# Masked attention over gathered tokens: each batch's token order made three batches ahead, beside the batch's mean, in place of all orders in the first batch

## The reference

```python
xt = jnp.transpose(x, (0, 2, 1))
qh = (xt @ Wq.T).reshape(B, T, 8, 64).transpose(0, 2, 1, 3)
scores = scale * jnp.einsum('bhqd,bhkd->bhqk', qh, qh)
logits = (scores * cmask + (1.0 - cmask) * NEG) * rmask
ctx = jnp.einsum('bhqk,bhkd->bhqd', jax.nn.softmax(logits, axis=-1), qh)
out = x + jnp.transpose(ctx.transpose(0, 2, 1, 3).reshape(B, T, D) @ Wo.T, (0, 2, 1))
```

## Time and profile before

| | before |
|---|---|
| median of 3 runs | 1604.44 us (1604.06 to 1607.05) |
| the profiled execution | 1601.72 us |
| its span, first to last instruction | 1599.9 us |
| instructions | 33099 |
| PE / DVE / ACT / POOL busy | 1526.0 / 1189.8 / 852.9 / 1340.2 us |
| share of the span | 95% / 74% / 53% / 84% |
| mean granted TensorE clock | 0.984 of 2.4 GHz |

### The profile page before, as it was taken

How to read it: one execution, slowest core, us unless ns; L and a number is a source line. 1 busy time by engine, 2 the same in 40 slices (tenths; PEclk the granted TensorE clock), 3 DMA queues, 4 the chain that set the end, 5 groups by cost and what they waited for, 6 DMA issues and landing times. The chain is left out here.

```text
span 1599.9 us, 33099 instructions
## 1 busy us (share of the span) xinstructions
PE 1526.0 (95%) x10956; PEld 1215.0 (76%) x10956; DVE 1189.8 (74%) x2676; ACT 852.9 (53%) x2061; POOL 1340.2 (84%) x1078
## 2 busy tenths in 40 slices
PE   5889999999999999999999999999999999999985
PEld 4668787777878777787777878778787877877763
DVE  4586787878778787877878787787877778787763
ACT  4335555565555556555555556556555555645451
POOL 3466889898998989889898988989898898988885
PEclk9879999999999999999999999999999999999998
DMA  4433454454544445444445544444544444443411
GB/s 137 104 78 90 101 126 103 129 124 110 127 105 122 107 130 123 111 120 112 116 112 130 124 106 119 114 119 113 129 121 108 116 118 119 112 125 93 113 58 55
DMA packets 93810, 179.09 MB, mean 112 GB/s; under 512 B 24704, under 2 KB 24832, under 8 KB 93632
## 3 DMA queue, kind: packets, MB, share of 16 engines
q1 hardware_dynamic: 64448, 109.71, 29.7%
q0 software_dynamic: 29184, 67.17, 14.8%
HBM read 36.77 MB, written 33.55 MB: 44 GB/s over the span
## 5 line engine op out<-in xcount | busy, mean ns | idle before, releaser
L977 DVE TENSOR_REDUCE small_mxp<-max_scores 108x1 f32<-108x270 f32 x1280 | 547.0, 435 | 267.2 <-PE max_scores L1218 244.5
L827 ACT ACTIVATE small_Pt<-scores,small_kbias 108x270 f32<-108x270 f32 x1280 | 550.5, 482 | 362.2 <-PE scores L1237 356.8
L640 POOL TENSOR_TENSOR small_Pacc<-small_Pacc,small_Pt 108x540 f32<-108x540 f32 x384 | 518.8, 1351 | 119.7 <-ACT small_Pt L827 113.2
L1218 PE MATMUL max_scores<-small_ops 128*108 128x270 f32 x1280 | 417.0, 332 | 17.1 <-DVE small_mxp L977 15.4
L1249 PE MATMUL ctx_psum<-small_Pt,small_V 108*64 108x270 f32 x2560 | 314.0, 392 | 0.0
L1009 DVE RECIPROCAL small_rsum<-small_rsum 128x67 f32<-128x67 f32 (+1 forms) x512 | 240.7, 532 | 70.3 <-ACT small_rsum L763 67.1
L1218 PEld LDWEIGHTS max_scores<-small_ops 128*108 128x108 f32 x1280 | 220.1, 174 | 86.6 <-issue 42.1
L1234 PE MATMUL scores<-small_ops 128*108 128x270 f32 x1280 | 271.0, 292 | 2.7 <-ACT small_Pt L827 2.7
L1249 PEld LDWEIGHTS ctx_psum<-small_Pt,small_V 108*64 108x64 f32 x2560 | 185.0, 138 | 107.9 <-issue 1.6
L1237 PE MATMUL scores<-small_ops 128*108 128x270 f32 x1280 | 265.4, 289 | 0.0
L1234 PEld LDWEIGHTS scores<-small_ops 128*108 128x108 f32 x1280 | 192.9, 174 | 21.8 <-issue 8.8
(11 more groups left out here) (130 smaller groups left out, 2386.9 us busy)
## 6 DMA issues: line engine op xcount, KB each, us to landing
small_ops<-small_H SPq DMA_DIRECT2D x512, 135.0 KB, 2.5
small_ops<-small_L SPq DMA_DIRECT2D x256, 135.0 KB, 2.5
small_ops<-small_mrow SPq DMA_DIRECT2D x128, 2.1 KB
small_xg<-x_rows,small_idx POOLq DMA_INDIRECT x80, 3.8
small_xtail<-x_rows,small_idx POOLq DMA_INDIRECT x80, 4.8
out_rows<-small_xtail,small_idx POOLq DMA_INDIRECT x80, 3.9
out_rows<-small_xg,small_idx POOLq DMA_INDIRECT x80, 3.8
wqT_sb<-wqT SPq DMA_DIRECT2D x1, 1024.0 KB, 5.4
```

The costliest lines, as they stand in the source:

```text
L640: nc.gpsimd.tensor_tensor(acc, other, t["Pt"][:R, p0], ALU.add).then_inc(pacc_step, 1)
L827: nc.scalar.activation(t["Pt"][:R, (NT * s + k) % f.NP, half, :], ST[(2 * (NT * h + k) + half) % 3][:R, 0:H], ACT.Exp, bias=t["kbias"][:R, ...
L977: nc.vector.tensor_reduce(t["mxp"][:R, h % 2, m // 2, m % 2:m % 2 + 1], MX[m % 2][:R, 0:H], AX.X, ALU.max).then_inc(mx_red, 1)
L1218: nc.tensor.matmul(MX[m % 2][:R, 0:H], ops[:, OPA, tile_cols(m // 2)], ops[:, OPB, half_cols(m % 2)], start=True, stop=True).then_inc(mx_r ...
```

## The change

For the small form (and the like "middle" one) the orders of batches 0, 1 and 2 are made in the front part, and that of batch b + 3 in batch b, for b = 0 to 12. VectorE makes the one-hots of that one batch (`hot_of`, four instructions) in step (5, 3), ahead of the second max block. TensorE's 8 matmuls stand in step (6, 2) just ahead of the mean `xbar`, in the same PSUM bank, at columns 8 to 17. VectorE makes `idx` in the step after it, once ScalarE has copied the mean out. The copied tables and the one-hots of all batches are gone, and ScalarE's wait for all orders with them. The instructions of ScalarE, GpSimd and SyncE and their order are the same as before.

```diff
-HOT_ROW_AT = [(0, 0), (0, 3), (1, 0), (1, 2), (1, 3), (1, 4), (2, 0), (2, 2), (2, 3), (2, 4), (3, 0), (3, 2), (3, 3), (3, 4)]
-ORDER_AT = [(0, 1), (0, 4), (1, 1), (1, 3), (1, 4), (2, 0), (2, 1), (2, 3), (2, 4), (3, 0), (3, 1), (3, 3), (3, 4), (4, 0)]
+HOT_AT = (5, 3)
+ORDER_COL = 8
...
             + ([("order", 1, 0)] if form.split else []) + [("proj", (1, 1), 0)]
+            + ([("order", 2, 0)] if form.split else [])
             + [("proj", (2, 0), 0), ("mT", 0, 0)])
...
-                        act.wait_ge(idx_made, B)
...
+                def hot_of(b):
 
                     shape = [P, TT, NTALL]
+                    at_least(dve, perm_made, b)
+                    nc.vector.scalar_tensor_tensor(out=t["jl"][:], in0=t["jh"][:, :, b], scalar=-float(R), in1=pos[:, :, b],
+                                                   op0=ALU.mult, op1=ALU.add).then_inc(place_step, 1)
+                    nc.vector.tensor_tensor(t["hot_tile_f"][:], t["tileno"][:].unsqueeze(1).to_broadcast(shape),
+                                            t["jh"][:, :, b].unsqueeze(2).to_broadcast(shape), ALU.is_equal).then_inc(place_step, 1)
+                    dve.wait_ge(place_step, NTALL + 4 + 2 * b)
+                    nc.vector.tensor_tensor(t["hot_tile"][:], t["hot_tile_f"][:],
+                                            tokid[:, :, b].unsqueeze(2).to_broadcast(shape), ALU.mult).then_inc(onehots_made, 1)
+                    nc.vector.tensor_tensor(t["hot_row"][:], t["rowno"][:].unsqueeze(1).to_broadcast([P, TT, R]),
+                                            t["jl"][:].unsqueeze(2).to_broadcast([P, TT, R]),
+                                            ALU.is_equal).then_inc(onehots_made, 1)
...
+                def idx_of(b, bank):
+
+                    dve.wait_ge(perm_made, b + 1)
+                    nc.vector.tensor_scalar(t["idx"][:R, b], bank[:R, ORDER_COL:ORDER_COL + NTALL], float(T * b), None,
+                                            ALU.add).then_inc(idx_made, 1)
...
+                    elif name == "xbar":
+                        dve.wait_ge(xbar_kept, b + 1)
+                        idx_of(b + 3, MB[bank])
...
-                    if f.split and (name, arg) == ("xT", NT - 1):
-                        move_tables()
-                    if f.split and (name, arg) == ("proj", (0, 0)):
-                        hot_tiles(t["late_hot_tile"])
                     if f.split and (name, arg) == ("proj", (0, 1)):
-                        hot_row_of(1)
+                        hot_of(1)
+                    if f.split and (name, arg) == ("proj", (1, 0)):
+                        hot_of(2)
...
-                                if f.split and not has_prev and a == 0 and (h, k) in HOT_ROW_AT:
-                                    hot_row_of(2 + HOT_ROW_AT.index((h, k)))
+                                if f.split and b + 3 < B and a == 0 and (h, k) == HOT_AT:
+                                    hot_of(b + 3)
...
+                def order_of(b, bank):
+
+                    pe.wait_ge(onehots_made, 2 * b + 2)
                     for tt in range(TT):
+                        last = nc.tensor.matmul(bank[:R, ORDER_COL:ORDER_COL + NTALL], t["hot_row"][:, tt, :],
+                                                t["hot_tile"][:, tt, :], start=(tt == 0), stop=(tt == TT - 1))
                     last.then_inc(perm_made, 1)
...
                         at_least(pe, xbar_kept, b + 1)
+                        if f.split and b + 3 < B:
+                            at_least(pe, idx_made, b + 4)
...
                     elif name == "xbar":
 
+                        if f.split and b + 3 < B:
+                            order_of(b + 3, mb)
                         pe.wait_ge(xsum_step, (NTALL - 1) * (b + 1))
```

More of the change, by code:

```diff
@@ L385, in attention_kernel @@
         tensors = [{} for _ in forms]
-        late_tables = []
         for f, t in zip(forms, tensors):
@@ L403, in attention_kernel, with place_tables @@
             keep("kbias", [P, B, f.NT], F32)
-            def place_tables(stage, t=t, f=f):
-                batches = 1 if f.split else B
+            def place_tables(t=t, f=f):
                 tables = ExitStack()
[L409 to L420, removed]
@@ new lines, in place_tables @@
+                for name, shape, dt in (
+                        ("tileno_i", [P, f.NTALL], I32), ("rowno_i", [P, f.R], I32), ("jidx_i", [P, f.NTALL], I32),
+                        ("boff_i", [P, B, f.NTALL], I32), ("boff", [P, B, f.NTALL], F32)) + (() if f.split else (
+                            ("jh", [P, TT, B], F32), ("jl", [P, TT, B], F32), ("tileno", [P, f.NTALL], F32),
+                            ("rowno", [P, f.R], F32), ("hot_tile_f", [P, TT, B, f.NTALL], F32),
+                            ("hot_tile", [P, TT, B, f.NTALL], F16), ("hot_row", [P, TT, B, f.R], F16))):
+                    t[name] = sb(f"{f.name}_{name}", shape, dt, tables)
@@ L964, in body @@
[L964 to L969 removed]
+                    hot_of(0)
@@ L1115, in batch @@
                                     reduce_max(s + 2, h + 2, 2 * k + a)
-                                done = [j for j in table[h, k] if j[1] in ("proj", "out", "xT", "order") and j[6]]
+                                done = [j for j in table[h, k] if (j[1] in ("proj", "out", "xT") or j[1] == "xbar" and f.split and b + 3 < B) and j[6]]
                                 due = [j for j in done if j[0] == 0] if a == 1 else late
@@ L1168, in order @@
                     last.then_inc(perm_made, 1)
-                def late_order(b, bank):
-                    pe.wait_ge(onehots_made, 3 + b)
+                def order_of(b, bank):
+                    pe.wait_ge(onehots_made, 2 * b + 2)
                     for tt in range(TT):
-                        last = nc.tensor.matmul(bank[:R, 0:NTALL], t["late_hot_row"][:, b % 2, tt, :],
-                                                t["late_hot_tile"][:, tt, b, :], start=(tt == 0), stop=(tt == TT - 1))
+                        last = nc.tensor.matmul(bank[:R, ORDER_COL:ORDER_COL + NTALL], t["hot_row"][:, tt, :],
+                                                t["hot_tile"][:, tt, :], start=(tt == 0), stop=(tt == TT - 1))
                     last.then_inc(perm_made, 1)
                 pe.wait_ge(consts_cast, 1)
-                pe.wait_ge(onehots_made, 2)
-                order(0, ST[0], slice(0, NTALL))
+                if f.split:
+                    order_of(0, ST[0])
+                else:
+                    pe.wait_ge(onehots_made, 2)
+                    order(0, ST[0], slice(0, NTALL))
                 def make_G(k, bank, rows):
```

67 lines of the change are left out of this document (25 added, 42 removed).

## The result

| | before | after |
|---|---|---|
| median | 1604.25 us (1603.96 to 1607.05) | 1690.43 us (1689.19 to 1692.35) |
| profiled execution's span | 1599.9 us | 1687.6 us |
| PE / DVE / ACT / POOL busy | 1526.0 / 1189.8 / 852.9 / 1340.2 us | 1541.3 / 1260.6 / 852.6 / 1335.1 us |
| mean granted TensorE clock | 0.984 | 0.966 |

The changed kernel is slower: the ratio is 1.0522, with a 95% interval of 1.0503 to 1.0542. The forecast was 1686 us. In the list of groups of the page after, one entry answers for the change: TensorE's idle time ahead of the max blocks, ended by VectorE's reduction. It was 17.1 us before.

The account below looks back on a forecast made before the run. Middle batches were taken as bound by TensorE's queue, batch 0's heads 1 to 3 by VectorE. Thirteen batches of 8.0 us (104) less 22.3 given back make 82 more: 1604.4 + 82 = 1686 us, range 1620 to 1714.

Parts of the forecast that it names:

- by turns: Step (5, 3): the four VectorE instructions alternate with GpSimd's additions, so TensorE waits 4.6 us, then 0.4: 5.0 a batch.
- rival 3: Step (5, 3): VectorE gets no turn until GpSimd has a gap; 2 us a batch more, 1712 us; chance 0.09.
- The sign that I had set for turns: The four instructions last 1.3 to 2.4 us where they take 0.2 to 1.0 alone, with GpSimd's additions between them.
- the row of 4.45 us: Batch 0's row one-hots, 4.45 us in place of 1.04; read as two GpSimd instructions running to their end ahead.
- Rival 2: Step (5, 3): only one or two of the four wait for GpSimd, 2.6 us less; 1615 to 1652 us; chance 0.17.
- The clock, 2.9 us: Behind TensorE's wait in each batch the clock falls; price between 0 and 3.7 us, taken as 2.9.
- Rival 1: By turns, but the clock stays up: 5.1 us a batch, 1648 us; chance 0.17.
- The order's matmuls, 0.5 us: Step (6, 2): 8 matmuls added to TensorE's full queue, 0.5 us in each of batches 0 to 12.
- Thirteen batches of 8.0: Batches 0 to 12 each get 0.5 + 5.0 - 0.4 + 2.9 = 8.0 us longer, 104 us in all.
- Batch 0, 21.3 us: Batch 0, heads 0 to 4: removing fourteen row one-hots and their matmuls gives back 21.3 us, bounds 14 to 25.
- The front part, 1.0 us: Front part: 1.8 us from the tile one-hots gone, less 0.8 for batch 2's order: net gain 1.0 us.
- Rival 4: No contention at all in step (5, 3): 1.6 us a batch, 1603 us; chance 0.14.

Follow-up runs that it names:

- e1: The changed kernel without its four VectorE instructions in the batches, matmuls and idx kept (later orders from batch 2's one-hots): 1588.46 us, ratio 0.9875 to the kernel before.
- e12: The changed kernel plus 36 trials of six GpSimd additions and a VectorE request, with no DMA issue, one right ahead, or one and a wait: 2039.22 us with trials.
- e5: The changed kernel with only the first, 8-number instruction of the four left at (5, 3): 1682.07 us, ratio 1.0463 to the kernel before.
- e9: e5 with its instruction replaced by a plain subtraction of 8 neighbouring numbers: 1683.4 us, ratio 1.0459 to the kernel before.
- e4: The changed kernel with the four instructions moved to the end of step (2, 2): 1595.44 us, ratio 0.9920 to the kernel before.
- e8: The kernel before plus 40 trials behind its last scatter, each six GpSimd additions and one VectorE subtraction of two SBUF tensors: 1916.63 us with trials.
- e2: The changed kernel with four reductions of one SBUF input and about the same lengths in place of the four instructions: 1598.87 us, ratio 0.9939 to the kernel before.
- e7: e4, but with the four instructions left at (5, 3) in batch 0: 1590.36 us, ratio 0.9888 to the kernel before.
- e10: e5 with its one instruction a tile sooner, at step (5, 2): 1588.49 us, ratio 0.9882 to the kernel before.
- e11: The changed kernel plus 40 trials of six GpSimd additions and one VectorE request of varied form, behind a reduction reading SBUF or PSUM: 1993.42 us with trials.

## Why the prediction was right, and where not

- **The side, the place and the size: right.** 1690.4 against 1686, and heads 5 and 6 grow by 8.8 us where "some 8 us" was forecast. e1 shows that the four instructions are the cause. The size is partly luck: a batch's wait was put 1.5 us too low, 0.4 us was let come back and didn't, and against these the clock was put 1.1 us too high and one batch too many was counted.
- **VectorE's wait, "by turns", 5.0 us: wrong in kind, undersized.** There are no turns at (5, 3). It is rival 3 in mechanism, which I had at 0.09 (its 1712 us is too high by the clock and the batch too many): 6.38 us for the first and no wait for the other three. The sign that I had set for turns, four instructions of 1.3 to 2.4 us each, is not there. TensorE waits 6.55 us (batch 5) in place of 4.6 + 0.4. The step that failed is the choice between the earlier trace rows. Both are real, and e12 shows what a reader of the trace has to look for: a DMA issue right ahead of the additions. The timeline of before had one, a scatter's issue, 0.02 us ahead of the first addition of the earlier trace rows:

```profile
607.88 1.00 POOL L586 DMA_INDIRECT out_rows<-small_xg,small_idx  x1 [0.19 <-issue]
```

  I counted the additions from 608.90 on and not what stood before them. Where the last batch goes by turns, there is no issue ahead. I also read the row of 4.45 us too low: not two but three GpSimd instructions, from 85.10 to 88.87 us, went ahead of it. Rival 2, that a small instruction slips past, is refuted by e5 and e9.
- **The clock, 2.9 us: oversized.** Behind the wait the lower level lasts to about 636.6: 0.50 of 1.34 us, 0.50 of 2.00 and 0.06 of 2.00 us make 1.8 us. 6.55 + 1.8 + 0.4 (matmuls) = 8.75, and heads 5 and 6 of batch 5 show 8.8. In e5 the wait is shorter, (81.6 - 18.9) / 12 = 5.2 us by the page's idle times of e5 and e1, and the batch still 7.7 us longer than in e1, so 2.5 us are left for the clock. The shorter wait has the higher price. Rival 1, a clock that stays up, is refuted.
- **The order's matmuls, 0.5 us: right.** e1 has 0.4 us a batch.
- **Thirteen batches of 8.0: twelve of 9.0.** In batch 0 GpSimd has a gap at (5, 3), and heads 5 and 6 together grow by 1.4 us only, 0.4 of it the matmuls. Batches 1 to 12 cost 107.4 us against 104 forecast for 13.
- **Batch 0, 21.3 us: right.** Its first five heads went from 71.15 to 51.0 us, so 20.2. Heads 1 to 3 came to 10.4, 9.9 and 10.0, not 9.6, and head 4 to 12.6. Their windows have the clock at 1.00 throughout, where it was 0.72 to 0.80.
- **The front part, 1.0 us: right as far as it can be told.** TensorE's wait for L is 1.04 us in place of 2.80, and this execution's front part is 3.5 us shorter. But the same front part took from 57.6 (e4) to 62.6 us (e9) in the profiles of experiments that don't touch it, and that of the kernel before 63.1 and 62.4 us (e8), so 3.5 isn't a measure of the edit.
- **Rival 4, faster: it did not happen at (5, 3), but where the wait is gone the change is faster.** It gave 1.6 us a batch and 1603 us. At the same place without the contention (e2) a batch costs 1.3 us; e7 has 0.8 us a batch (94.4 against 93.6) and 1590 us, where the kernel before took 1608.6 beside it.

Left open: the row of 4.45 us lost two ends of additions with no DMA issue seen ahead, the addition before having followed 3.33 us of idle time. Why an issue ahead makes the difference isn't shown, nor how short a gap between it and the additions is enough; 2.5 to 2.7 us was in e12. A version of the changed kernel with such a gap at (5, 3) was not tried.

## What to carry to other kernels

Before a small VectorE instruction with two SBUF inputs is put on a path that TensorE waits for, read what GpSimd has queued from there to its next gap, and whether a DMA issue stands right ahead of it: the price is that whole stretch and not the instruction's 0.16 us. If so, move it by a tile (94 us here, e5 to e10) or into a GpSimd gap, and in a batch with other work look for the place anew, as e7 did. A probe that reproduces a stall only when one more ingredient is put in tells more about its cause than another look at the kernel that has it.

## What was unexpected in the hardware

- Behind a GpSimd DMA issue with additions right after it, VectorE's request stayed out for all of them, in 12 trials of 12 (5.19 to 6.13 us); with none, or with a gap of 2.5 to 2.7 us between, it got the next turn in 24 of 24 (0.21 to 1.15 us), and in 80 of 80 in e8 and e11. The Trainium skill (SBUF — State Buffer, Who interferes with whom) has the second to issue blocked until the first finishes. The 104 cases agree with that; the 12, and the 6.38 us of the changed kernel, don't.
- A GpSimd DMA issue takes part in this too: in e10 one lasts 1.68 us, from 209.13, in place of 1.0, beside a VectorE subtraction of two SBUF tensors (0.71 us, from 209.24). In the trace of before all 14 issues in which such a subtraction of 540 numbers begins last 1.63 to 1.70 us, and the 187 that no VectorE instruction with two inputs touches last 0.94 to 1.17.
- A 540-number VectorE subtraction that gets its turn makes the next GpSimd addition 1.74 us long in place of 1.26.
